# Attention and expert layer on one core: the first four tiles prepared in two pieces of two instead of three of one, one and two

## The reference

```python
x = x + global_latent_attn(rmsnorm(x, norm1_w), g_wq, g_kv_down, g_k_up, g_v_up, g_wo)   # causal
x = x + local_gqa_attn(rmsnorm(x, norm2_w), l_wq, l_wk, l_wv, l_wo)                      # window of 32
x = layernorm(hidden + x)
# experts: 1 shared, 8 routed, the best 2 of 8 for each token
shared = silu(xt @ sg_w.T) * (xt @ su_w.T) @ sd_w.T
probs = sigmoid(xt @ router_w.T + routing_bias)
topk_p, topk_idx = top_k(probs, 2); topk_p = topk_p / sum(topk_p)
y = einsum(silu(einsum(xt, wg)) * einsum(xt, wu), wd)
out = layernorm(x + shared + einsum(w, y))
```

## Time and profile before

| | |
|---|---|
| median of three runs | 706.99 us (706.08 to 707.47) |
| the profiled execution, its own time | 701.55 us |
| span of the profiled execution | 699.7 us |
| mean granted clock of TensorE over the span | 0.981 |
| busy: PE, DVE, ACT, POOL | 613.1, 492.5, 431.7, 374.7 us |

### The profile page before, as it was taken

The page is one execution under the profiler, slowest core; times in us unless marked ns, Lnnn a source line. Parts: engine busy times, 40 slices in busy tenths (PEclk is TensorE's granted clock), DMA queues, the critical chain, the costliest instruction groups (busy, mean ns, idle before and its releaser), DMA issues. The chain is left out here.

```text
span 699.7 us, 12475 instructions
## 1 busy us (share of the span) xinstructions
PE 613.1 (88%) x4017; PEld 326.7 (47%) x4017; DVE 492.5 (70%) x1332; ACT 431.7 (62%) x597; POOL 374.7 (54%) x430
## 2 busy tenths in 40 slices
PE   2589989899999999999899999999979999899950
PEld 1233233344444345444244434457666776576850
DVE  3656786767986598977679797387757577245773
ACT  4586988777777877667875648444714544343433
POOL 3466655636433645433423777723774557777822
PEclk9999999999999999999999999999999999999995
DMA  9346307800000010000000011100022331436162
GB/s 260 146 156 218 125 2 220 280 4 2 2 5 1 1 18 6 12 5 16 16 1 6 17 43 33 47 8 3 7 83 69 83 83 52 116 94 196 42 191 60
DMA packets 56558, 47.76 MB, mean 68 GB/s; under 512 B 27392, under 2 KB 53664, under 8 KB 55840
## 3 DMA queue, kind: packets, MB, share of 16 engines
q1 hardware_dynamic: 45408, 35.63, 17.5%
q0 software_dynamic: 4352, 9.05, 3.8%
q10 hardware_dynamic: 6736, 2.30, 1.2%
HBM read 35.29 MB, written 28.98 MB: 92 GB/s over the span
## 5 line engine op out<-in xcount | busy, mean ns | idle before, releaser
L945 ACT ACTIVATE prob<-ps_s 128x1024 f32<-128x1024 f32 x320 | 308.7, 1025 | 103.6 <-PE ps_s L1303 67.3
L1345 PE MATMUL ps_v<-prob,va 128*32 128x512 f32 x1152 | 153.1, 612 | 3.6 <-POOL prob L833 2.9
L1303 PE MATMUL ps_s<-qs,ks 32*128 32x512 f16 x576 | 103.5, 390 | 23.3 <-ACT prob L945 15.7
L1588 POOL DMA_INDIRECT y_rows<-y,to_row x72 | 70.0, 972 | 39.4 <-DVE y L1709 21.8
L1303 PEld LDWEIGHTS ps_s<-qs,ks 32*128 32x128 f16 x576 | 25.4, 91 | 134.9 <-ACT prob L945 85.0
L833 POOL TENSOR_SCALAR_AFFINE_SELECT prob<-prob 128x1024 f32<-128x1024 f32 x64 | 69.7, 1108 | 23.6 <-ACT prob L945 23.1
L1094 DVE STREAM_TRANSPOSE sums<-ps_v 128x512 f32<-128x512 f32 x62 | 44.2, 713 | 52.7 <-PE ps_v L1339 30.8
L1621 ACT ACTIVATE gated<-ps_gu 128x512 f32<-128x512 f32 x46 | 27.5, 597 | 76.9 <-PE ps_gu L1816 63.3
L1816 PE MATMUL ps_gu<-weights,rows_t 128*128 x144 | 68.0, 594 | 0.0
L1339 PE MATMUL ps_v<-prob,vd 128*128 128x256 f32 (+1 forms) x292 | 58.9, 349 | 2.1 <-DVE marked L1115 1.5
L1339 PEld LDWEIGHTS ps_v<-prob,vd 128*128 128x128 f32 x292 | 49.3, 191 | 13.5 <-issue 4.6
(11 more groups left out here) (231 smaller groups left out, 1051.1 us busy)
## 6 DMA issues: line engine op xcount, KB each, us to landing
x_rows<-in_blank SPq DMA_DIRECT2D x8, 2112.0 KB, 9.8
rows<-x_rows SPq DMA_DIRECT2D x72, 66.0 KB
chosen_y<-y_rows SPq DMA_DIRECT2D x8, 512.0 KB, 6.0
weights<-in_weights SPq DMA_DIRECT2D x1, 3456.0 KB, 13.6
vd<-v_rows SPq DMA_DIRECT2D x128, 4.0 KB
out<-result ACTq DMA_DIRECT2D x8, 256.0 KB, 2.2
marked<-in_hidden SPq DMA_DIRECT2D x3, 512.0 KB, 5.5
r_in<-in_hidden SPq DMA_DIRECT2D x6, 256.0 KB, 2.9
```

The source lines that it names most:

```text
L945: act.activation(probs_at(n, 0, SLOT_COLS), scores_at(n, 0, SLOT_COLS), ACT.Exp, scale=HD ** -0.5 / GAIN ** 2).then_inc(exped, 1)
L1303: last = pe.matmul(scores_at(n, j * BANK, BANK).rearrange("p (r q) -> p r q", r=REP), ks[b % QUERY_BATCHES][rows, kt * P:(kt + 1) * P], qs ...
L1345: last = pe.matmul(bank[g * VW:(g + 1) * VW, :, :], va[b % VALUE_BATCHES][:, kt, g, :], probs_at(n + g // 2, g % 2 * BANK, BANK).rearrange ...
L1588: pool.indirect_dma_start(y_rows, bass.IndirectOffsetOnAxis(ap=to_row[:, m, t:t + 1], axis=0), y[m][:, t, :], None).then_inc(y_sent[half_o ...
```

## The change

The first four tiles are prepared as two chunks of two tiles, (0, 0, 0) and (0, 0, 2), where there were three, of one, one and two. Their starts are steps -40 and -36 (before -40, -37, -32), and the chunk of tiles 4 to 7 starts at step -30 (before -27). The pause of two steps that stood ahead of tile 1 now stands ahead of tile 2, so the slots of tile 1 come two steps earlier and all later slots keep their steps. By the rule above the next chunks start at -16, -2, 11 and 23 (before -13, 1, 14 and 26); from the chunk (1, 0, 4) at step 52 on all starts are as they were.

Products of zeros: 29 places with 155 products become 23 places with 159. A chunk number in a key is one lower for the same chunk from (0, 0, 4) on. Removed are ('weigh', 9), ('weigh', 37), those at the scores 97, 138, 168, 177, 188 and 248, and those at two turns of parts in the first half, one turn of tokens and one turn of parts in the second. Added are those at the scores 3, 8, 29 and 34, at turn_tokens 5 and at wo 7; wo 2 gets 16 in place of 3. The others are as they were.

```diff
--- before.py
+++ after.py
@@ -116,10 +116,10 @@
 LOCAL_OFFSETS = {3: [2], 4: [2], 5: [1, 9], 6: [1, 6], 7: [2, 7]}
 LOCAL_INSIDE = {(b, qt): offsets for b in range(1, B) for qt, offsets in LOCAL_OFFSETS.items()} | {(B - 1, TPB - 1): [2, 6, 10, 14]}
 FIRST_STEP = -29
-PAUSES = {(1, 3, 4): 40, (0, 0, 1): 2, (0, 0, 4): 2}
-CHUNK_ORDER = [(0, 0, 0), (0, 0, 1), (0, 0, 2), (0, 0, 4), (0, 1, 0), (0, 1, 4), (1, 0, 0), (0, 2, 0), (1, 0, 4), (0, 2, 4),
+PAUSES = {(1, 3, 4): 40, (0, 0, 2): 2, (0, 0, 4): 2}
+CHUNK_ORDER = [(0, 0, 0), (0, 0, 2), (0, 0, 4), (0, 1, 0), (0, 1, 4), (1, 0, 0), (0, 2, 0), (1, 0, 4), (0, 2, 4),
                (1, 1, 0), (0, 3, 0), (1, 1, 4), (0, 3, 4), (1, 2, 0), (1, 2, 4), (1, 3, 0), (1, 3, 4)]
-SMALL = {(0, 0, 0): 1, (0, 0, 1): 1, (0, 0, 2): 2}
+SMALL = {(0, 0, 0): 2, (0, 0, 2): 2}
 ...
 PREPARE_STEPS = 36
@@ -130,7 +130,7 @@
 PLACES = (-0.5, -0.25, 0)
 START_DELAYS = {(1, 3, 4): 3, (0, 2, 4): 2, (1, 0, 0): -1, (1, 0, 4): 8, (1, 1, 4): -3, (0, 2, 0): -2, (1, 2, 4): -2}
 SPACING = 14
-FIRST_STARTS = (-40, -37, -32, -27)
+FIRST_STARTS = (-40, -36, -30)
 PREPARE_SMALL = [(0, "square"), (1, "sum"), (1, "invert"), (1, "refine"), (2, "scale"), (3, "turn_tokens"), (3, "move_tokens"),
                  (4, "project", 0), (4, "rotate", 0), (5, "add"), (5, "square_heads"), (6, "sum_heads"), (6, "invert_heads"),
                  (7, "normalise"), (7, "split_heads"), (8, "pair_parts"), (9, "turn_parts", 2), (9, "move_parts", 2),
@@ -162,7 +162,7 @@
 FILL_END = [(1, 'fill_down', 2), (2, 'fill_down', 3), (0, 'fill_moved', 2), (1, 'fill_moved', 3), (2, 'fill_down', 4), (2, 'fill_down', 5), (2, 'fill_moved', 4), (2, 'fill_moved', 5), (6, 'fill_added', 2), (6, 'fill_added', 3), (8, 'fill_added', 4), (10, 'fill_added', 5)]
 
 
-WARM = {('wo', 2): (3, 0), ('turn_parts', 3, 2): (3, 0), ('weigh', 9): (3, None), ('weigh', 37): (7, 0), ('score', 97): (2, 0), ('turn_parts', 10, 2): (3, 0), ('score', 138): (2, 0), ('score', 168): (2, 0), ('score', 177): (2, 0), ('route_turn', 0): (5, 0), ('score', 188): (2, 0), ('turn_tokens', 14): (3, 0), ('project', 14, 0): (8, 1), ('score', 248): (2, 0), ('choose_rank', 3): (8, 0), ('weigh', 136): (3, 1), ('score', 265): (15, 0), ('weigh', 149): (3, 0), ('weigh', 150): (9, 0), ('wo', 50): (3, 0), ('score', 308): (4, 0), ('wo', 57): (4, 0), ('weigh', 170): (4, 0), ('wo', 59): (7, 0), ('turn_tokens', 17): (10, 0), ('fill_gate', 4): (12, 0), ('turn_parts', 17, 2): (3, 0), ('score', 316): (7, 1), ('wo', 63): (7, 0), ('turn_parts', 2, 2): (9, 0)}
+WARM = {('score', 8): (8, 1), ('wo', 2): (16, 0), ('score', 29): (3, 0), ('score', 34): (4, 0), ('turn_tokens', 5): (3, 0), ('wo', 7): (10, 0), ('route_turn', 0): (5, 0), ('project', 13, 0): (8, 1), ('choose_rank', 3): (8, 0), ('weigh', 136): (3, 1), ('score', 265): (15, 0), ('weigh', 149): (3, 0), ('weigh', 150): (9, 0), ('wo', 50): (3, 0), ('score', 308): (4, 0), ('wo', 57): (4, 0), ('weigh', 170): (4, 0), ('wo', 59): (7, 0), ('turn_tokens', 16): (10, 0), ('fill_gate', 4): (12, 0), ('score', 316): (7, 1), ('wo', 63): (7, 0), ('score', 3): (6, 1)}
 
 
 class Steps:
```

## The result

The changed kernel takes 709.62 us (median of 20 runs, 705.34 to 714.76). The kernel before, timed beside it, takes 706.35 us (median of 20, 702.61 to 709.11). The ratio of after to before is 1.0048, 95% interval 1.0030 to 1.0065: slower by about half a per cent. 710.0 us was predicted, with 703.5 to 714.5 as the range. The profiled execution of the new kernel takes 709.48 us, with a span of 707.5 us and a mean granted clock of 0.976 (before: 701.55, 699.7 and 0.981).

The account below looks back on a forecast made before the run. PE was taken as the bound, with ACT close behind until 130 us. Tile 4's delay +2.5, later products +0.5, removed products 0 and clock 0 gave +3.0 on the median 706.99: 710.0 us, range 703.5 to 714.5.

Parts of the forecast that it names:

- The first score at 24.7: Start of the kernel: with two tiles prepared at once, the first score starts at 24.7 us, 3.3 us later than 21.42.
- Slot 6 on ACT at 42.7, the head inversion at 48.4: ACT before tile 4: slot 6 is 2.8 us behind; the head inversion of tiles 4 to 7 follows at 48.4, against 50.20.
- the faster rival: At wo 2: tile 2's sums come before the pairs are ready, tile 4 starts 2.3 us earlier, 704.4 us; chance 20%.
- `wo` 2 held by DVE until 55.7, with the 16 products lying inside: Before tile 4: wo 2 waits for DVE's split, token sum and tile 2's sums; 16 products (3.5 us) fit in, until 55.6.
- Tile 4 at 63.3, net +2.5: Tile 4 starts 3.1 us later than 60.20; 0.6 back for a turn of tokens formerly done after its start.
- From tile 4 on, +0.5: Second term: chunks three steps earlier cost nothing; 13 more products between tiles 4 and 8 cost 0.5 of 0 to 2.8 us.
- Products removed further on, 0: From score 97 on: without six pairs of products the scores wait longer for the same exponential; gain 0, at most 2.6 us.
- The clock, left as it is: Whole run: early rise unchanged or below 1 us; low stretches near 410 us and some 27 us later stay, 1.7 us each.
- "more low clock" rival: Products in the middle gone: the clock falls one to three times more, 1.7 us each, 713.4 at two falls; chance 12%.
- the distance at 130 us isn't the distance at the end: Sign of a wrong prediction: the two traces lie a different time apart at 130 us than at the end.
- The sum: Whole kernel: 2.5 + 0.5 + 0 + 0 = +3.0 us, added to the runs' median of 706.99; forecast 710.0, chance 46%.

Follow-up runs that it names:

- clear_early: The change with the four clearings of kd and vd on ACT moved to earlier steps, ahead of slot 0; ratio to before 1.0018.
- clear_early_next: The change with early clearings on ACT, the chunks behind tile 4 at before's starts, and 9 products at wo 2 instead of 16; 701.91 us, ratio 0.9957.
- after_again: The change itself, unchanged, run again for a second profile; 706.95 us beside 706.30 for before, ratio 1.0029.
- next_chunks_restored: The change with the four chunks behind tile 4 back at before's starts (-13, 1, 14, 26), products as in the change; 705.98 us, ratio 1.0025.
- products_alone: The kernel before, with its three pieces, given the change's products of zeros; 716.00 us beside 704.75 for before, ratio 1.0152.
- pieces_alone: The change's two pieces and starts, with the products of zeros of the kernel before; 710.22 us beside 704.75 for before, ratio 1.0105.
- middle_restored: The change with the 21 products of zeros put back that it removed from score 97 on; 709.42 us, ratio 1.0048.

## Why the prediction was right, by its steps

- *The first score at 24.7*: 24.72. The rotation was put at 12.5 and came at 12.65; the head sum at 15.2 and came at 15.87, so part of the agreement is errors that cancel; the second piece's projection stands ahead of the queries' turn, as the prediction had it.
- *Slot 6 on ACT at 42.7, the head inversion at 48.4*: 42.45 and 47.87. The point that was to decide between the forecast and the faster rival (under 40 or over 42) fell on the forecast's side. clear_early shows that the clearings ahead of slot 6 are a cause of it: moved away, they take 1.6 us with them to the end.
- *`wo` 2 held by DVE until 55.7, with the 16 products lying inside*: 55.81; with 3 products it is 55.92. The token sum of the next chunk in between was counted, and clear_early_next, which takes it and the clearings away, has `wo` 2 at 53.04. The 55.81 is in part luck: the head inversion came 0.5 us before its forecast and the conversion behind it took 0.8 us more than in before. In after_again DVE is done at 53.71 and the products hold `wo` 2, so "fit in there" is true of one profile and not of the other.
- *Tile 4 at 63.3, net +2.5*: 63.05, net 2.85 - 0.6 = +2.25.
- *From tile 4 on, +0.5*: this is the term that was mis-sized. The distance at 162 is 4.03, so it measured 4.03 - 2.25 = 1.8. Two parts of it have a price in other kernels. "PE has it in its queue either way, so I cost it at nothing" was wrong by 0.7: next_chunks_restored, with the old starts, has 3.3. The products, taken as 0.5, cost 1.0 in before's order (products_alone, next_chunks_restored). That they sum to 1.7 is no proof of the 1.8, for in the change's own order the first ten cost nothing until 107 us (pieces_alone). How the 1.8 divides in the change itself stays open.
- *Products removed further on, 0*: right. At score 97 the wait took their place, as the row of after shows beside the earlier trace rows (0.80 us in place of 0.60 of products and 0.26 of waiting), and middle_restored has the same ratio as the change. The prediction priced six pairs and didn't name the nine products of the three turns; they are in middle_restored too.

```profile
155.71 0.39 PE L1303 MATMUL ps_s<-qs,ks 32*128 32x512 f16 x2 [0.80 <-ACT prob L945]
```

- *The clock, left as it is*: not shown wrong on the mean of many runs (0.9745 against 0.9747, though those of before are of other chips; side by side on one chip 0.9785 against 0.9741), in the profiled execution wrong. It has four low stretches between 250 and 610 us where before's has two, which is the "more low clock" rival in that one execution, and brings its distance from 4 to 8 us. One sign of being wrong that the prediction names is that the distance at 130 us isn't the distance at the end. By that sign it failed: 3.94 at the addition at 132 us of before and 7.8 at the end, and 4.4 to 5.8 in after_again.
- *The sum*: +3.0 was predicted for the medians and +3.3 came out. The order alone costs 4.0 by the trace and 4.2 ± 0.6 at equal clock, so the small error of the total hides the 1 us that the second term was short of. The 710.0 also starts from a median of before, 706.99 of three runs, that was 0.64 above the 706.35 of twenty; this made up for the 0.27 by which the difference was short and more. Both are luck. Adding the difference to the median, and not taking the profile's own 701.55 as the level, was needed: the profiles differ by 7.9 us, the medians by 3.3. The profile of before was simply one of its better executions.

The rival on the other side, tile 4 coming early, needed three more edits. clear_early_next makes them, and tile 4 is then on time, though not early.

## What to carry to other kernels

When two small pieces of preparation become one, count the late first result, but then look at what else now stands in the row ahead of the work that the bound engine waits for: here a buffer clearing on ACT (1.6 us) and a token sum on DVE came to stand in front of it, the one because its steps weren't moved along, the other because its start moved along by rule. With both put right, tile 4 was on time in spite of the late first score. Filler products are to be chosen with the order and not by themselves: the new set cost 7.3 us at equal clock in the old order. And where the clock falls now and then, don't compare two single profiles by their spans; compare a mark that comes ahead of the falls, and the times at equal clock.
